# Moving one unit's value products behind other work in TensorE's order, in a two-layer Perceiver-like block

## The chip, the cores and the metric

The kernel runs on 1 core of one Trainium2 chip. The metric is the device time of one execution in microseconds (us). Three executions of the kernel before took 1425.46, 1426.5 and 1429.1 us, a median of 1426.5 us.

## The reference, cut to what matters

The input is 128 batches of 32 tokens of width 256, with a context of 257 keys per batch. Six sub-layers follow each other, each on a layer norm of the running sum and each added to it. Only the names matter below:

```
x = x + cross_attention_0(norm(x), ctx)     # "cross0", one head, 257 keys
x = x + self_attention_0(norm(x))           # "self0", causal, 32 keys
x = x + quantised_feed_forward(norm(x))     # "ffn", 256 -> 1024 -> 256, gelu
x = x + cross_attention_1(norm(x), ctx)     # "query1"/"x1": 16 heads of 16, 257 keys
x = x + local_attention(norm(x))            # "self1": window of 5 among 32 keys
x = x + routed_experts(norm(x))             # "router", then 8 experts, 2 per token
```

The last layer counts tokens per expert in token order and drops those over a capacity. The kernel therefore first writes a table in DRAM that says which token stands where in which expert's queue, and then works off the queues in blocks of 128 rows.

## The kernel before, in words

**Tiles.** Four batches of 32 tokens make a tile of 128 rows, and there are 32 tiles. `stack_phase` takes all tiles through the first five layers and through the router. `expert_phase` then runs the experts and is not touched.

**Units.** The sixteen-head cross-attention of a tile is worked in four units, one for each batch of the tile. For each unit TensorE makes scores (`unit_scores`, L1252, 16 products), VectorE their row maxima (`unit_max`, L1788), ScalarE the exponentials (`unit_probs`, L1426), TensorE the transposes of these (`unit_probs_T`, L1260), ScalarE their copy to SBUF (L1430), and TensorE the value products (`unit_values` and `values_of`, L1263 to L1283: 64 pairs of a weight load and a product on the line L1271, each product only 17 columns wide). Then VectorE adds the last key's part (`unit_own`, L815) and inverts the row sums (`unit_inverse`, L821), GpSimd scales (`unit_scaled`, L933), and VectorE turns the block (`unit_turned`, L825). The units are numbered 0 to 3, so "the fourth unit" is unit 3.

**The order is written out by hand.** Every engine has a function `slot(s)`, which is unrolled for every s in `SLOTS`, and which lists the steps of this engine for several tiles at once: `at(s + 2, step)` does the step for tile s + 2. A round of TensorE holds 505 products in its steady state. Engines meet only at semaphores; `W(engine, signal, tile, step)` waits for one, and each engine works strictly in its own order. The slots are in L1285 (TensorE), L1444 (ScalarE), L1583 (GpSimd) and L1820 (VectorE). `W_bank` waits until the readers of a PSUM bank are done.

**Banks around the change.** Unit 2's values go to bank 6, unit 3's to bank 5. Bank 6 is taken by `c0_norm_T` (L1096, product line L1100) after `unit_own(s, 2)`. Bank 5 is taken by `s0_norm_T` (L1163, product line L1167) after `unit_own(s, 3)`. `s1_v_scores` (L758) makes the second self-attention's value product (line L714, `w_a_Wv`) and its scores (line L765) in bank 7, and needs `ff_gelu1` of tile s + 2 to be done there.

**GpSimd's order.** In its slot stand one after the other `unit_scaled` for units 2 and 3, `scatter_behind` (L1568, L1591; in some of the slots it issues two indirect DMAs from `write_entry`, line L1566, that write a tile's entries of the table), `unit_last(0)` (L1550, `x_lastv`), two bias additions (L913), `ro_rstd` (L923, L1595; `inverse_std`, lines L907 and L909), another bias addition for cross0 (L913).

**Who waits for it.** VectorE's `ro_norm` (L871, line L797, at L1868 in the slot) needs `ro_rstd`. It stands ahead of `s1_x5` and of `s1_x` (L827, line L830, at L1872). `s1_x` frees bank 4 for TensorE's `ro_logits` (L779, at L1288, line L714 with `router`), which stands third in TensorE's next slot, ahead of the next scores:

```
def ro_logits(t):
    W(pe, act_s["router"], t, "normT")
    W_bank(pe, (t + 3, (dve_s["self1_in"], "x")), ...
```

and the quantiser's scale on VectorE, which the change moves too, is

```
def ff_hidden_scale(t):
    W(dve, act_s["ffn"], t, "gelu1")
    row_scale("ffn", t, 1, hid)      # L1740, L1742, L1744, L1745
```

Of the kernel before, what the change touches and what calls it, by code (L numbers as in the profile page):

```python
# [490 lines left out]
def stack_phase(nc, first, t_in, const, logits, ps, constants, consts_loaded, zero, contexts, w2, w2_in, table, table_in, tab_i, places, places_in, rt,  # L491
# [206 lines left out]
    def at(t, step, *unit):  # L698

        name = step.__name__  # L700
        left = CLOSING.get(name, int(name in ("unit_own", "unit_inverse", "unit_scaled", "unit_turned") and unit[0] >= 2))
        if 0 <= t < tiles - left:
            step(t, *unit)
# [256 lines left out]
    with nc.Block() as block:  # L960
# [88 lines left out]
        def _(pe):  # L1049
# [235 lines left out]
            def slot(s):  # L1285
                at(s, unit_probs_T, 1, 1)
                at(s + 1, ff_hidden_T)
                at(s - 4, ro_logits)  # L1288
                at(s + 2, s0_scores)
                at(s, unit_scores, 2)  # L1290
                at(s + 3, c0_scores)
                at(s, unit_values, 0)
                at(s + 1, ff_down)
                at(s, unit_probs_T, 2, 0)
                route_counts(s - 1)
                at(s + 3, c0_probs_T)
                at(s + 2, s0_values)
                at(s, unit_probs_T, 2, 1)
                at(s + 2, s0_out)
                at(s, unit_scores, 3)  # L1300
                at(s + 1, q1_norm_T)
                at(s + 3, c0_values)
                at(s, unit_values, 1)
                at(s + 1, q1_q)
                at(s - 1, s1_norm_T)
                at(s + 3, c0_att_T)
                at(s - 3, ro_norm_T)
                at(s, unit_probs_T, 3, 0)
                at(s, unit_probs_T, 3, 1)
                at(s + 3, c0_out)  # L1310
                at(s + 2, ff_in_T)
                at(s - 1, s1_q)
                at(s + 2, ff_up0)
                at(s + 2, ff_up1)
                at(s + 1, unit_scores, 0)
                at(s, unit_values, 2)
                at(s, unit_values, 3)
                at(s - 1, s1_v_scores)
                at(s + 4, c0_norm_T)
                at(s + 1, unit_probs_T, 0, 0)  # L1320
                at(s + 3, s0_norm_T)
                at(s + 1, unit_probs_T, 0, 1)
                at(s + 4, c0_q)
                at(s + 1, unit_scores, 1)
                at(s + 3, s0_qkv)
                at(s, s1_out)
                at(s - 1, s1_values)
                at(s + 1, unit_probs_T, 1, 0)

            for s in SLOTS:  # L1330
                slot(s)
# [282 lines left out]
        def _(dve):  # L1614
# [180 lines left out]
            def routing(s, j):  # L1795

                first_turn = [rv.best, rv.shifted, rv.first_key, rv.first_top, rv.first_hot, rv.rest, rv.second, rv.second_key]
                second_turn = [rv.second_rank, rv.second_top, rv.second_hot, rv.run_0, rv.run_1, rv.run_2, rv.run_3, None]
                third_turn = [rv.sum, rv.share, rv.where, rv.second_share, rv.held, rv.kept, rv.both, rv.gate]
                fourth_turn = [rv.both_columns, rv.address, rv.address_sum, rv.whole, rv.column, rv.column_f, rv.place, None]  # L1800
                for turn, steps in enumerate((first_turn, second_turn, third_turn, fourth_turn)):
                    g = group_at(s, turn)
                    if g is not None and steps[j]:
                        if steps[j] == rv.where and g == IN_FIRST - 1:
                            next(first_table)
                        steps[j](g, *GROUPS[g])
                        if steps[j] == rv.where:
                            rv.carry(g, *GROUPS[g])
                if (s, j) > (TOTAL_AT, 2) and (s, j) < (TABLE_AT, 2):
                    next(first_table, None)  # L1810
                if (s, j) == (TABLE_AT, 2):
                    rv.rows(0, bank(B["rw"]), tab_i[0])

            def first_from(u):
                if u == 0:
                    dve.wait_ge(places_in[0], 16)
                column = dve.value_load(tab_i[0][0:1, bass.ds(u + P, 1)], min_val=0, max_val=EXP * tiles)
                v_.tensor_copy(first.from_ix[u][:], places[0][:, column, 0:1]).then_inc(first.from_ok.handle, 1)

            def slot(s):  # L1820
                at(s, unit_own, 0)
                at(s + 1, ff_x)
                at(s, unit_inverse, 0)
                at(s + 1, q1_moments)
                routing(s - 1, 2)
                at(s + 3, c0_inv)
                at(s - 1, s1_norm)
                at(s, unit_turned, 0)
                at(s + 1, q1_norm)
                at(s + 2, s0_x)  # L1830
                at(s, unit_max, 3, 0)
                at(s + 2, ff_moments)
                at(s, unit_max, 3, 1)
                at(s + 3, c0_att)
                at(s, unit_own, 1)
                at(s + 2, ff_norm)
                at(s, unit_inverse, 1)
                routing(s - 1, 3)
                at(s + 2, ff_quantise_in)
                at(s + 4, c0_norm)  # L1840
                at(s + 3, c0_x)
                routing(s - 1, 4)
                at(s + 3, s0_moments)
                at(s + 5, c0_moments)
                at(s, unit_turned, 1)
                at(s - 1, s1_qT)
                at(s + 3, s0_norm)
                at(s + 1, unit_max, 0, 0)
                at(s + 1, unit_max, 0, 1)
                at(s, unit_own, 2)  # L1850
                at(s, unit_own, 3)
                at(s, unit_inverse, 2)
                at(s, unit_inverse, 3)
                at(s + 2, ff_hidden_scale)
                at(s, unit_turned, 2)
                at(s - 1, s1_masked)
                if s == tiles - 2:
                    first_from(0)
                    first_from(1)
                at(s + 2, ff_quantise_hidden)  # L1860
                at(s + 1, unit_max, 1, 0)
                at(s, unit_turned, 3)
                at(s - 1, s1_turned)
                routing(s - 1, 5)
                at(s + 1, unit_max, 1, 1)
                at(s - 1, s1_inv)
                routing(s - 1, 6)
                at(s - 2, ro_norm)  # L1868
                at(s - 1, s1_x5)
                routing(s - 1, 7)  # L1870
                routing(s, 0)
                at(s, s1_x)  # L1872
                at(s, s1_moments)
                at(s - 1, ro_moments)
                at(s - 3, ro_logits)
                routing(s, 1)
                at(s + 3, s0_masked)
                at(s + 1, unit_max, 2, 0)
                at(s + 1, unit_max, 2, 1)
                at(s + 4, c0_max)  # L1880
                at(s + 3, s0_scaled)

            for s in SLOTS:
                slot(s)
# [522 lines left out]
```

## Time and profile before

| what | value |
|---|---|
| median of three executions | 1426.5 us |
| the profiled execution | 1423.56 us |
| its span, first to last instruction | 1421.7 us |
| mean granted TensorE clock | 0.985 |
| busy: TensorE / its weight loads | 95% / 80% |
| busy: VectorE, ScalarE, GpSimd | 61%, 55%, 46% |
| TensorE's first and last value product (L1271) | 80.7 us, 882.1 us |

The profile is of one execution. Its own time is 1.9 us over its span, which lies around the span, and 2.9 us under the median of the three. Shares of busy time are means over two phases. From about 60 to 890 us the stack phase runs, in which four engines work side by side; after it the experts' products fill TensorE alone. The change lies in the first.

### The profile page before, as it was taken

Reading aid. Unit: us, or ns where it says so; the run is one execution under the profiler, and the core shown is the slowest. Engines: PE = TensorE matmul, PEld = TensorE weight load, DVE = VectorE, ACT = ScalarE, POOL = GpSimd, SP = SyncE. Lnnn points to the kernel's source line nnn. Section 1 sums busy time; section 2 is a strip of 40 time slices with the busy share of each in tenths; the row PEclk is TensorE's granted clock in tenths of the full one; section 3 lists DMA queues with packets and bytes.
Section 4 is the critical chain, followed back from the end, with each engine's and each line's share of the span. In section 5 each row is a group of like instructions: output and inputs, shape, how many; then the busy total and the mean of one; then the engine's idle time right before and its main releaser. Section 6 shows DMA issues by size and latency. Waiting matters only on the chain. (4 is left out here: it accounts for less than half of the span.)

```text
span 1421.7 us, 51433 instructions
## 1 busy us (share of the span) xinstructions
PE 1344.6 (95%) x19870; PEld 1133.9 (80%) x19903; DVE 863.1 (61%) x3111; ACT 780.4 (55%) x1855; POOL 647.8 (46%) x1195
## 2 busy tenths in 40 slices
PE   8789999999999988999999978999999999999996
PEld 6467777777777767777777756899999999999995
DVE  5679999999988878899999965333111111111110
ACT  1588888888877777888888865321111111111111
POOL 1234444443454545554555543466544434443442
PEclk9899999999999999999999988999999999999999
DMA  9424444343433333343333314666666666666662
GB/s 328 162 75 117 124 114 125 106 125 105 120 117 93 115 111 98 103 134 105 115 108 106 112 69 149 220 182 186 174 178 178 188 182 180 184 184 184 181 181 56
DMA packets 91179, 201.77 MB, mean 142 GB/s; under 512 B 13568, under 2 KB 48128, under 8 KB 79840
## 3 DMA queue, kind: packets, MB, share of 16 engines
q1 hardware_dynamic: 72304, 176.97, 38.4%
q0 software_dynamic: 15680, 18.69, 7.4%
q10 hardware_dynamic: 2992, 3.28, 0.7%
q8 instruction: 142, 2.33, 0.7%
q14 instruction: 61, 0.50, 0.1%
HBM read 180.88 MB, written 18.29 MB: 140 GB/s over the span
## 5 line engine op out<-in xcount | busy, mean ns | idle before, releaser
L2165 ACT ACTIVATE heT<-ps 128x512 f32<-128x512 f32 x142 | 84.7, 597 | 412.0 <-PE ps L2091 383.5
L2091 PEld LDWEIGHTS ps<-xeT,w_block 128*128 128x128 f32 x2272 | 264.6, 192 | 3.7 <-issue 0.2
L2091 PE MATMUL ps<-xeT,w_block 128*128 128x128 f32 x2272 | 266.1, 275 | 0.0
L2078 PE MATMUL ps<-contexts,heT 128*128 x1136 | 257.5, 379 | 1.6 <-DVE ye L1972 1.6
L1426 ACT ACTIVATE x_prob<-ps,x_nmax 128x257 f32<-128x257 f32 x512 | 210.7, 473 | 67.3 <-DVE x_nmax L1788 64.3
L2078 PEld LDWEIGHTS ps<-contexts,heT 128*128 128x128 f32 x1136 | 210.1, 190 | 27.5 <-issue 2.0
L1788 DVE TENSOR_REDUCE x_nmax<-ps 128x2 f32<-128x514 f32 x256 | 169.2, 682 | 15.8 <-PE ps L1252 14.1
L1260 PE MATMUL ps<-constants,x_prob 128*128 128x128 f32 x1024 | 153.1, 281 | 8.4 <-ACT x_prob L1426 7.2
L1430 ACT ACTIVATE x_probT<-ps 128x512 f32<-128x512 f32 x256 | 147.0, 622 | 10.6 <-PE ps L1260 6.3
L1971 DVE COPY to_ix<-places 128x1 uint32 x71 | 10.9, 154 | 231.5 <-PE ps L2078 223.0
L2206 POOL TENSOR_TENSOR rt_hold<-constants 128x1 f32<-128x1 f32 x143 | 34.4, 240 | 225.3 <-DVE ye L1972 124.2
L1260 PEld LDWEIGHTS ps<-constants,x_prob 128*128 128x128 f32 x1024 | 120.1, 144 | 21.0 <-ACT x_prob L1426 14.4
L933 POOL TENSOR_TENSOR x_scaled<-x_own,x_rinv 128x64 f32<-128x64 f32 x128 | 36.3, 294 | 207.4 <-DVE x_rinv L821 207.0
L2212 POOL DMA_INDIRECT out<-ye,to_ix x71 | 113.0, 1591 | 28.5 <-issue 24.0
L1271 PEld LDWEIGHTS ps<-contexts,x_probT 128*32 128x32 f32 x8192 | 90.2, 110 | 39.7 <-ACT ffn_hidden L1396 15.2
L1271 PE MATMUL ps<-contexts,x_probT 128*32 128x17 f32 x8192 | 93.1, 186 | 12.3 <-issue 10.8
L1252 PE MATMUL ps<-contexts,query_blocks 32*64 32x257 f32 x2048 | 89.0, 403 | 11.3 <-ACT x_probT L1430 8.9
L1990 DVE COPY xeT<-ps 128x256 f32<-128x256 f32 x71 | 30.1, 424 | 85.5 <-PE ps L2069 85.4
L2209 POOL DMA_INDIRECT xe<-xnorm,from_ix x69 | 69.0, 1000 | 22.4 <-issue 20.3
L1550 POOL TENSOR_TENSOR x_lastv<-contexts,x_prob 128x68 f32<-128x68 f32 x128 | 44.1, 344 | 60.7 <-ACT x_prob L1426 60.3
L1252 PEld LDWEIGHTS ps<-contexts,query_blocks 32*64 32x64 f32 x2048 | 30.2, 130 | 44.4 <-ACT x_probT L1430 28.1
L907 POOL TENSOR_TENSOR self_var_eps<-self_moments,epsilon 128x1 f32<-128x1 f32 x64 | 12.1, 189 | 88.9 <-DVE self_moments L793 88.9
(280 smaller groups left out, 2714.4 us busy)
## 6 DMA issues: line engine op xcount, KB each, us to landing
w_block<-in_m_w SPq DMA_DIRECT2D x71, 1024.0 KB
contexts<-in_cn SPq DMA_DIRECT2D x112, 272.0 KB
contexts<-in_cT SPq DMA_DIRECT2D x112, 257.0 KB
contexts<-in_m_w SPq DMA_DIRECT2D x8, 1024.0 KB
contexts<-in_cn SPq DMA_DIRECT2D x4, 1088.0 KB
contexts<-in_lastk SPq DMA_DIRECT2D x32, 136.0 KB
contexts<-in_cT SPq DMA_DIRECT2D x4, 1028.0 KB
xin<-in_x SPq DMA_DIRECT2D x32, 128.0 KB, 2.1
```

Of the source, the lines that this page charges most:

```text
L1252: i = mm(ps[h * HS:(h + 1) * HS, r, 0:KEYS], qblk[t % 2][r * GD:(r + 1) * GD, h, u, :, :].rearrange("p e q -> p (e q)"), cT[t % RING][r * ...
L1260: i = tr(ps[:, r, n * P:(n + 1) * P], p1[u % 2][:, r, n * P:(n + 1) * P], ident[:])
L1271: i = mm(b[rows_of, r * DH1:(r + 1) * DH1], p1T[u % 2][:, r, n, rows_of], cn_heads[t % RING][:, u, n, column, :], start=n == 0, stop=n == ...
L1426: A(p1[u % 2][:, r, :], ps[:, r, 0:KEYS], ACT.Exp, bias=nmax1[u % 2][:, r:r + 1]).then_inc(e1_ok.handle, 1)
L1430: A(p1T[u % 2][:, 2 * j:2 * j + 2].rearrange("p r k t -> p r (k t)"), ps[:, 2 * j:2 * j + 2, 0:KT * P], ACT.Copy).then_inc(t1_ok.handle, 1)
L1550: tt(lastv[u % 2][:].rearrange("p (r d) -> p r d", r=RG), lastk[t % RING][:, u, :].rearrange("p (r d) -> p r d", r=RG), p1[u % 2][:, :, KE ...
L1788: v_.tensor_reduce(nmax1[u % 2][:, 2 * j:2 * j + 2], ps[:, 2 * j:2 * j + 2, 0:KEYS], AX, ALU.max, negate=True).then_inc(m1_ok.handle, 1)
L2078: t = mm(ps[:, 3, 0:D], heT[b][:, k, :], w2[:, e, k, :], start=k == 0, stop=k == FK - 1)
L2091: t = mm(ps[:, half, at:at + P], w1[b][:, k, f * P:(f + 1) * P], xeT[b][:, k, :], start=k == 0, stop=k == H - 1)
L2165: A(heT[b][:, half * FK // 2:(half + 1) * FK // 2, :].rearrange("p k t -> p (k t)"), ps[:, half, :], ACT.Gelu).then_inc(heT_ok.handle, 1)
L2209: g.indirect_dma_start(xe[b][:], None, sources[round_of(u, n)], bass.IndirectOffsetOnAxis(ap=from_ix[b][:], axis=0)).then_inc(xe_in[b], 16)
L2212: g.indirect_dma_start(sums[round_of(u, n)], bass.IndirectOffsetOnAxis(ap=to_ix[b][:], axis=0), ye[b][:], None, compute_op=ALU.add).then_i ...
```

## The change

In TensorE's slot unit 3's values stand three steps later, behind `s1_v_scores` and `c0_norm_T`. In VectorE's slot the quantiser's scale of the hidden layer, `ff_hidden_scale`, stands earlier, between `unit_own` of unit 2 and `unit_own` of unit 3, where it stood behind both `unit_own` and both `unit_inverse`. Nothing is added or removed, and GpSimd, ScalarE and the DMA queues keep their order.

```
--- before.py
+++ after.py
@@ -1314,9 +1314,9 @@
                 at(s + 2, ff_up1)
                 at(s + 1, unit_scores, 0)
                 at(s, unit_values, 2)
-                at(s, unit_values, 3)
                 at(s - 1, s1_v_scores)
                 at(s + 4, c0_norm_T)
+                at(s, unit_values, 3)
                 at(s + 1, unit_probs_T, 0, 0)
                 at(s + 3, s0_norm_T)
                 at(s + 1, unit_probs_T, 0, 1)
@@ -1848,10 +1848,10 @@
                 at(s + 1, unit_max, 0, 0)
                 at(s + 1, unit_max, 0, 1)
                 at(s, unit_own, 2)
+                at(s + 2, ff_hidden_scale)
                 at(s, unit_own, 3)
                 at(s, unit_inverse, 2)
                 at(s, unit_inverse, 3)
-                at(s + 2, ff_hidden_scale)
                 at(s, unit_turned, 2)
                 at(s - 1, s1_masked)
                 if s == tiles - 2:
```

## Rows read from the trace of the kernel before

**Rows 1.** DMA queues from 113.95 to 803.72: packets, MB, share of 16 engines.
```profile
q8 instruction: 109, 1.79, 1.0%
```

**Rows 2.** Four stretches: length, busy time (instructions) per engine, granted clock, DMA.
```profile
113.95:286.50 172.55, 169.03 (x3526) 133.12 (x3534) 158.15 (x534) 146.81 (x370) 81.43 (x181) 1.00 0.40 117
286.50:387.27 100.77, 96.98 (x2026) 77.23 (x2029) 91.86 (x336) 85.34 (x214) 45.91 (x105) 1.00 0.39 115
387.27:604.62 217.35, 198.86 (x4050) 157.29 (x4057) 185.87 (x671) 171.55 (x427) 110.19 (x227) 0.98 0.35 108
604.62:803.72 199.10, 195.43 (x4052) 154.23 (x4059) 186.80 (x685) 170.44 (x427) 106.21 (x225) 1.00 0.35 109
```

**Rows 3.** The third of them, L1201 alone (two products per round), PE's first.
```profile
387.27:604.62 217.35, 2.21 (x16) 0.91 (x17) 0.98 0.35 108
```

**Rows 4.** The fourth of them, L1566 alone: GpSimd's scatters, busy (count).
```profile
604.62:803.72 199.10, 16.67 (x16) 1.00 0.35 109
```

**Rows 5.** Waits of PE from 387.27 to 604.62: us in total, times, longest.
```profile
PE ps L1271 <- issue: 9.3, 6, 1.9
```

**Rows 6.** Timeline of PE, 525.4 to 532: start, us, instructions, [idle before <-releaser].
```profile
525.45 0.69 PE L1252 MATMUL ps<-contexts,query_blocks 32*64 32x257 f32 x16
526.18 1.25 PE L1271 MATMUL ps<-contexts,x_probT 128*32 128x17 f32 x116
529.03 0.31 PE L1271 MATMUL ps<-contexts,x_probT 128*32 128x17 f32 x12 [1.61 <-issue]
```

**Rows 7.** DMA from 526.5 to 527.8 in 40 slices, the instruction queue's one packet alone.
```profile
GB/s 0 504 0 0 0 0 0 0 0 0 0 0 0 0 0 0 0 0 0 0 0 0 0 0 0 0 0 0 0 0 0 0 0 0 0 0 0 0 0 0
```

**Rows 8.** Timeline of PE around the last such gap, 580.9 to 583.3.
```profile
583.07 0.38 PE L1271 MATMUL ps<-contexts,x_probT 128*32 128x17 f32 x23 [0.89 <-issue]
```

**Rows 9.** Timeline of PE in an undisturbed round, 187.5 to 194.2.
```profile
190.44 1.33 PE L1271 MATMUL ps<-contexts,x_probT 128*32 128x17 f32 x128
191.70 1.13 PE L714 MATMUL ps<-w_a_Wv,self_normT 128*128 128x256 f32 x4
...
193.30 0.63 PE L1260 MATMUL ps<-constants,x_prob 128*128 128x128 f32 x4
193.77 0.38 PE L1167 MATMUL ps<-constants,self_norm 128*128 128x128 f32 x2
```

**Rows 10.** Timeline of DVE in the round of rows 9.
```profile
191.93 0.35 DVE L815 TENSOR_TENSOR x_own<-ps,x_lastv 128x68 f32<-128x68 f32 x2
...
192.41 1.19 DVE L1740 TENSOR_REDUCE ffn_absmax<-ffn_hidden 128x1 f32<-128x1024 f32 x1
...
194.01 0.23 DVE L825 STREAM_TRANSPOSE x_outT<-x_scaled 128x64 f32<-128x64 f32 x1
```

**Rows 11.** Timeline of POOL, 655 to 667, a round with scatters.
```profile
659.23 0.55 POOL L933 TENSOR_TENSOR x_scaled<-x_own,x_rinv 128x64 f32<-128x64 f32 x2 [1.84 <-DVE x_rinv L821]
...
662.46 0.74 POOL L1550 TENSOR_TENSOR x_lastv<-contexts,x_prob 128x68 f32<-128x68 f32 x1
...
664.85 0.57 POOL L909 TENSOR_TENSOR router_rstd<-router_var_eps,minus_half 128x1 f32<-128x1 f32 x1
...
666.47 0.30 POOL L1550 TENSOR_TENSOR x_lastv<-contexts,x_prob 128x68 f32<-128x68 f32 x1 [0.36 <-ACT x_prob L1426]
```

**Rows 12.** Timeline of all engines, 615 to 618, another such round.
```profile
615.05 0.57 POOL L909 TENSOR_TENSOR router_rstd<-router_var_eps,minus_half 128x1 f32<-128x1 f32 x1
...
615.60 0.71 POOL L913 TENSOR_TENSOR cross_x_bias<-xin,r_x_bv 128x256 f32<-128x256 f32 x1
...
615.72 0.75 DVE L797 TENSOR_SCALAR x_norm<-x,router_moments,router_rstd 128x256 f32<-128x256 f32 x1
...
617.14 0.42 DVE L830 TENSOR_TENSOR x<-ps,x_bias 128x256 f32<-128x256 f32 x1
...
617.71 0.47 PE L714 MATMUL ps<-router,router_normT 128*128 128x8 f32 x3
```

**Rows 13.** Timeline of PE, 764 to 768: a wait that the trace shows.
```profile
767.08 0.58 PE L714 MATMUL ps<-router,router_normT 128*128 128x8 f32 x4 [0.23 <-DVE x L830]
```

More of the change, by code:

```diff
@@ L1316, in slot @@
                 at(s, unit_values, 2)
-                at(s, unit_values, 3)
                 at(s - 1, s1_v_scores)
                 at(s + 4, c0_norm_T)
+                at(s, unit_values, 3)
                 at(s + 1, unit_probs_T, 0, 0)
@@ L1850, in slot @@
                 at(s, unit_own, 2)
+                at(s + 2, ff_hidden_scale)
                 at(s, unit_own, 3)
@@ L1853, in slot @@
                 at(s, unit_inverse, 3)
-                at(s + 2, ff_hidden_scale)
                 at(s, unit_turned, 2)
```

## The prediction
> **What bounds the kernel now.** I read the busy times of stretches first, then TensorE's waits, then the timelines of single rounds. In the stack phase TensorE is busy 98% of 113.95 to 286.50 us and again of 604.62 to 803.72 us [rows 2]. It is TensorE's own order that bounds these rounds. The stretch from 387.27 to 604.62 has 8 rounds (two products of L1201 in each [rows 3]), and the last one, with the same number of products, has 8 too [rows 2]. There a round takes 199.10 / 8 = 24.89 us. The eight rounds before it take 217.35: 18.2 us more for the same work, at a granted clock of 0.98 instead of 1.00, so a little of it at the lower level of 1.2 GHz [rows 2].
>
> That surplus has a place. Six times TensorE stands idle inside the value products of units 2 and 3, 9.3 us in all, and no semaphore ended it [rows 5]. In one such round 116 of the 128 products run, then there is a gap of 1.61 us, then 12 [rows 6]; in the last of the six the gap comes ahead of the last 23 [rows 8]: it creeps through the code from round to round, as a fixed count of instructions would. I read it as a refill of the instruction stream. From 113.95 to 803.72 the instruction queue moves 109 packets of 1.79 MB in all, 16.4 KB each [rows 1], for 13,654 products and 13,679 weight loads [rows 2]: 251 in a packet, and I take 256, since TensorE's waits are not in these rows. One packet starts at 526.53, behind the values' start at 526.18, and TensorE goes on at 529.03 [rows 6, 7]. Counting back 256 instructions from there (232 in the 116 pairs, the rest in the scores ahead) one comes to about 525.5. So a block takes about 3.5 us from the moment its predecessor is entered, and TensorE used up a block in 527.43 - 525.5 = 1.9 us. The two units back to back are 256 instructions in 1.33 us [rows 9]. Nothing else in a round is so dense.
>
> **What the change does to the gaps.** The products between the two units take 193.30 - 191.70 = 1.60 us for 44 instructions [rows 9]. The densest 256 instructions are then unit 2 (0.65), these (1.60) and two thirds of unit 3 (0.43): 2.7 us against 1.3. Where a block begins ahead of unit 2, as in the six rounds of [rows 5], the 0.73 from the scores to the values comes on top in part, 3.3 us against 3.5. (That 0.73 is 526.18 - 525.45 [rows 6].) The gap that is left, 0.2 us, comes ahead of unit 3's end, where VectorE is not ready before 0.3 later (below). The other two rounds keep some 0.6 each. I take 1.2 us as left of 18.2, so **17.0 us go**. Bounds: 9.3 (the visible gaps alone) and 18.2. From 286.50 to 387.27 four rounds have milder gaps, 100.77 against 4 x 24.70, and their blocks begin inside unit 2, where 0.8 us stays; **-0.5**.
>
> The Trainium skill (Runtime: NRT & Kernel Launch, section Instruction fetch mechanics) says that code is refilled in blocks of 16 KiB, two held at a time, and that the fetch is hidden since issue is slower than the fill. The block size agrees with [rows 1]. That it is hidden does not, by the 1.61 us gap. By that sentence the gaps are something else and the 17.0 us stay.
>
> **What it costs at the same place.** VectorE now does the scale of the hidden layer between the two `unit_own`. That is 194.01 - 192.41 = 1.60 us [rows 10]. So `unit_own(3)`, both inverses and what GpSimd waits for come 1.60 later than now. Unit 3's products end 2.9 us after unit 2's start (0.65 + 1.60 + 0.65), that is 193.34 in the round of [rows 9], and `unit_own(3)` starts at 191.93 + 0.14 + 1.60 = 193.67 [rows 10] (0.14 is its distance from the first now), so the scale hides them with 0.3 us to spare. `s0_norm_T` wants bank 5 at 193.77 [rows 9]; `unit_own(3)` ends at 193.88, plus a tenth for the signal: TensorE waits 0.2. Part of that is taken up by ScalarE's chain behind it, but `unit_turned(2)` now waits for GpSimd a little. I take 0.2 per round, between 0 and 0.35, for the 11 rounds from 113.95 to 387.27: **+2.2 us**. `s1_v_scores`, now straight behind unit 2, needs the second gelu, which is done while unit 2 runs: nothing, and if it is late its 0.1 or less shows there.
>
> **What it costs later.** This is the large term. In the 16 rounds with a pair of scatters' issue (16 issues in the last stretch's 8 rounds [rows 4], and as many in the one before) GpSimd is full. It starts scaling at 659.23 and comes to `x_lastv` at 662.46, 3.23 later, and from there to the end of `router_rstd` it takes 2.96, or 2.5 if `x_lastv` takes its 0.30 and not 0.74 [rows 11]. Starting 1.60 later, `router_rstd` ends at 666.6 to 667.0 instead of 665.42. In [rows 12] `ro_norm` begins 0.10 behind that end already now, so there is no slack. It takes 0.75 beside the bias addition that GpSimd starts at 615.60. `s1_x` follows, and TensorE's router product comes 617.71 - 615.62 = 2.09 behind the end of `router_rstd`. For the round of [rows 11] this is 666.6 + 2.0 = 668.6 at the middle of it, against 665.42 + 2.1 = 667.5 now. TensorE already waits for `s1_x` there, 0.23 us [rows 13], and the next scores, maxima and exponentials are behind it, so the delay is paid in full. **1.0 us per round**; from 0.5 (`ro_norm` not held up) to 1.5 (`x_lastv` held up too and 2.09 throughout). With the round after 803.72, 17 rounds: **+17.0 us**. Rounds without scatters have GpSimd free at that point and pay nothing of this.
>
> The rule of the Trainium skill (SBUF — State Buffer, section SBUF: two separate sides) on the port pair that VectorE and GpSimd share, the later one blocking until the first is done, agrees with the 0.75 beside the 0.71 of GpSimd.
>
> **The end of the phase** has one more gap in unit 2 or 3; I take -1.0, from -2 to +1.
>
> **Sum:** -17.0 - 0.5 + 2.2 + 17.0 - 1.0 = +0.7 us. The profiled execution would take 1423.56 + 0.7 = 1424.3, the median 1426.5 + 0.7 = **1427.2 us**. About 0.3%, 4.3 us, is what a measurement of this kernel can tell from no change, so I forecast no difference.
>
> **Rivals.**
> - *The delay on GpSimd costs half.* The gaps go, and `ro_norm` runs unhindered, 0.5 per round: 1427.2 - 8.5 = **1418.7**. For it: the router's product of [rows 11]'s round came 2.1 behind `router_rstd` with the same steps between, so some of them waited for something else. Against: [rows 12, 13]. Chance 0.27.
> - *The router's chain takes the place of the gaps, at 1.5.* VectorE's and GpSimd's operations block each other in the new alignment; from 1.25 us per round this decides, and 17 x 0.5 more gives 1427.2 + 8.5 = **1435.7**, slower. For it: the bias addition is one of several that can collide. Against: `x_lastv` takes 0.30 elsewhere [rows 11]. Chance 0.19.
> - *The change doesn't do what it should: the gaps stay.* If they are no refill, or a refill needs far over 3.5 us, 17.0 stays: 1427.2 + 17.0 = **1444.2**; with half of it, 1435.7. For it: the packet's start [rows 7] explains 1.0 of the 3.5 us, and I don't see the rest. Against: the count of 256. Chance 0.10.
> - *The forecast,* both large terms within 4 us of each other: chance 0.44.
>
> **The numbers.** Faster 0.27, same 0.44, slower 0.19 + 0.10 = 0.29. Both signs hold over half, so the likeliest case's own range is 1423 to 1431. The range of 8 in 10 takes in the first two rivals' values: 1418 to 1435.5, with less than 2 in 10 outside, the third rival most of it.
>
> **What the profile after would show.** Right: rounds from 387 on of one length, about 25.9 us; no idle time of 1.5 us at L1271, `issue` waits of a few tenths at most; a new wait of TensorE for VectorE `x` L830 of about 1 us in every round with scatters, and `router_rstd` ending 1.1 to 1.6 later than now; early rounds of 24.9 us instead of 24.7; `s0_norm_T` (L1167) waiting 0.2 us for `x_own`. Wrong: rounds with scatters near 25.2 (first rival), or over 26.2 (second); gaps of a microsecond moved elsewhere (third); or a wait for ScalarE's exponentials that I costed at nothing, since `s1_masked` comes later on VectorE.

## The result and the profile after

The changed kernel takes 1437.34 us, a median of four executions (1435.88 to 1438.1), beside 1425.98 for the kernel before in the same runs. The ratio is 1.0079, with a 95% interval of 1.0054 to 1.0104. I forecast 1427.2, no difference, and a range up to 1435.5. It became slower, and the range missed it.

The head of the profile page of the changed kernel:

```profile
span 1436.3 us, 51465 instructions
PE 1356.5 (94%) x19902; PEld 1132.2 (79%) x19903; DVE 874.2 (61%) x3111; ACT 780.6 (54%) x1855; POOL 640.7 (45%) x1195
```

The busy times of its four stretches, which answer to [rows 2]: length, busy time and instructions of PE, PEld, DVE, ACT and POOL, granted clock, DMA share, GB/s. A round runs from one first product of L1201 to the next, and I number them, so that these stretches are rounds 2 to 8, 9 to 12, 13 to 20 and 21 to 28:

```profile
116.96:293.24 176.28, 171.94 (x3532) 133.50 (x3533) 161.49 (x534) 147.41 (x371) 81.34 (x181) 1.00 0.41 114
293.24:396.06 102.82, 99.01 (x2031) 77.49 (x2029) 94.49 (x336) 85.45 (x214) 46.65 (x105) 1.00 0.39 113
396.06:607.32 211.26, 199.35 (x4058) 155.31 (x4057) 188.06 (x671) 171.26 (x427) 104.32 (x227) 1.00 0.37 110
607.32:818.16 210.84, 200.81 (x4060) 155.61 (x4059) 187.89 (x685) 170.62 (x427) 103.77 (x225) 0.99 0.34 103
```

Against [rows 2] the stretches are 3.73, 2.05, -6.09 and 11.74 us longer. Another 3.01 us lie ahead of round 2, which begins at 116.96 and not at 113.95. In the thirteen traces of this case beside the changed one it begins anywhere from 112.57 to 118.78, whatever the order of the loop, so I count nothing of these 3 us to the change. After round 28 it is 0.16. That makes the 14.6 us between the two spans. The medians are only 11.4 us apart, since the profiled execution of the kernel before was 2.4 us under the median of its four.

TensorE's waits in the third and in the fourth stretch (us in total, times, longest), to be held against [rows 5]:

```profile
PE ps L714 <- DVE x_outT L825: 4.2, 6, 0.7
PE ps L1271 <- issue: 2.5, 5, 1.1
...
PE ps L714 <- DVE x_outT L825: 4.1, 6, 0.7
PE ps L1260 <- ACT x_prob L1426: 2.2, 4, 1.0
PE ps L714 <- DVE x L830: 2.1, 4, 0.8
```

The gaps at L1271 shrank from 9.3 us to 2.5. In their place TensorE waits for VectorE and ScalarE: 8.4 us in the fourth stretch, where all its waits came to 1.2 before, and 7.4 in the third, where it had waited 3.9 for ScalarE and nothing for VectorE. Before, these rounds were bound by TensorE; now VectorE with GpSimd sets them.

The early rounds show the plainest part of it. These are the groups of three VectorE lines in rounds 4 to 8, before and then after (durations in ns min/median/max, first and last start):

```profile
L1750 DVE TENSOR_SCALAR ffn_hidden<-ffn_hidden,ffn_qscale x5: 771/772/776, 170.2 to 269.0; 128x1024 f32<-128x1024 f32 x5
L1752 DVE TENSOR_SCALAR ffn_hq<-ffn_hidden x5: 1098/1102/1104, 171.0 to 269.8; 128x1024 bf16<-128x1024 f32 x5
L854 DVE TENSOR_TENSOR self_probT<-self_prob_turned,constants x5: 629/633/634, 172.9 to 271.7; 128x128 f32<-128x128 f32 x5
```

```profile
L1750 DVE TENSOR_SCALAR ffn_hidden<-ffn_hidden,ffn_qscale x5: 1253/1254/1261, 174.2 to 275.2; 128x1024 f32<-128x1024 f32 x5
L1752 DVE TENSOR_SCALAR ffn_hq<-ffn_hidden x5: 1096/1100/1103, 175.5 to 276.5; 128x1024 bf16<-128x1024 f32 x5
L854 DVE TENSOR_TENSOR self_probT<-self_prob_turned,constants x5: 634/636/639, 177.5 to 278.5; 128x128 f32<-128x128 f32 x5
```

L1750 went from 0.77 to 1.25. The timelines of GpSimd and then VectorE at that place of the changed kernel (start, us) show why:

```profile
199.46 0.73 POOL L913 TENSOR_TENSOR x_bias<-x,r_x_bo 128x256 f32<-128x256 f32 x1
200.15 1.18 POOL L913 TENSOR_TENSOR self_x_bias<-x,r_a_bv 128x256 f32<-128x256 f32 x1
...
199.49 1.25 DVE L1750 TENSOR_SCALAR ffn_hidden<-ffn_hidden,ffn_qscale 128x1024 f32<-128x1024 f32 x1
200.78 1.10 DVE L1752 TENSOR_SCALAR ffn_hq<-ffn_hidden 128x1024 bf16<-128x1024 f32 x1
```

GpSimd's addition begins 0.03 ahead of L1750, the second addition waits for L1750, and L1752 waits for the second addition. Each holds the other up. In the kernel before the addition began half a microsecond ahead of L1750, and cost it 0.03 at most (0.77, against 0.74 in e4 below):

```profile
194.35 0.73 POOL L913 TENSOR_TENSOR x_bias<-x,r_x_bo 128x256 f32<-128x256 f32 x1
...
194.86 0.77 DVE L1750 TENSOR_SCALAR ffn_hidden<-ffn_hidden,ffn_qscale 128x1024 f32<-128x1024 f32 x1
```

### The profile page after: what moved, and what is told of

The parts are those of the page before. It is cut to its first block and busy times, and to the rows that moved or that the text cites. A ratio compares the mean times of both kernels' runs of the same rounds, so it can differ in the third digit from the quotient of the medians.

```text
span 1436.3 us, 51465 instructions
## 1 busy us (share of the span) xinstructions
PE 1356.5 (94%) x19902; PEld 1132.2 (79%) x19903; DVE 874.2 (61%) x3111; ACT 780.6 (54%) x1855; POOL 640.7 (45%) x1195
## 3 DMA queue, kind: packets, MB, share of 16 engines
q8 instruction: 142, 2.33, 0.7%
## 5 line engine op out<-in xcount | busy, mean ns | idle before, releaser
L1260 PE MATMUL ps<-constants,x_prob 128*128 128x128 f32 x1024 | 153.5, 279 | 12.8 <-ACT x_prob L1426 11.4
L1260 PEld LDWEIGHTS ps<-constants,x_prob 128*128 128x128 f32 x1024 | 118.4, 143 | 25.6 <-ACT x_prob L1426 20.3
L1271 PEld LDWEIGHTS ps<-contexts,x_probT 128*32 128x32 f32 x8192 | 92.0, 110 | 38.7 <-ACT ffn_hidden L1396 15.3
L1271 PE MATMUL ps<-contexts,x_probT 128*32 128x17 f32 x8192 | 98.0, 186 | 6.3 <-issue 4.6
L1252 PE MATMUL ps<-contexts,query_blocks 32*64 32x257 f32 x2048 | 89.6, 405 | 6.7 <-ACT x_probT L1430 4.8
L1252 PEld LDWEIGHTS ps<-contexts,query_blocks 32*64 32x64 f32 x2048 | 30.2, 131 | 38.7 <-ACT x_probT L1430 20.3
L1550 POOL TENSOR_TENSOR x_lastv<-contexts,x_prob 128x68 f32<-128x68 f32 x128 | 40.9, 319 | 35.3 <-ACT x_prob L1426 34.8
```

The costliest lines, as they stand in the source:

```text
L1252: i = mm(ps[h * HS:(h + 1) * HS, r, 0:KEYS], qblk[t % 2][r * GD:(r + 1) * GD, h, u, :, :].rearrange("p e q -> p (e q)"), cT[t % RING][r * ...
L1260: i = tr(ps[:, r, n * P:(n + 1) * P], p1[u % 2][:, r, n * P:(n + 1) * P], ident[:])
L1271: i = mm(b[rows_of, r * DH1:(r + 1) * DH1], p1T[u % 2][:, r, n, rows_of], cn_heads[t % RING][:, u, n, column, :], start=n == 0, stop=n == ...
L1550: tt(lastv[u % 2][:].rearrange("p (r d) -> p r d", r=RG), lastk[t % RING][:, u, :].rearrange("p (r d) -> p r d", r=RG), p1[u % 2][:, :, KE ...
```

## The experiments

Three groups of kernels ran, four in each, and each group beside its own runs of the kernel before: 1420.9 us (19 runs), 1418.93 (16) and 1423.86 (25). So ratios are compared, and stretches of rounds within the profiles.

**One part of the change at a time.**

```
# e1: TensorE's part alone            # e2: VectorE's part alone
 at(s, unit_values, 2)                 at(s, unit_own, 2)
-at(s, unit_values, 3)                +at(s + 2, ff_hidden_scale)
 at(s - 1, s1_v_scores)                at(s, unit_own, 3)
 at(s + 4, c0_norm_T)                  at(s, unit_inverse, 2)
+at(s, unit_values, 3)                 at(s, unit_inverse, 3)
                                      -at(s + 2, ff_hidden_scale)
```

> TensorE's move alone, VectorE's order as before. Theory A (the gaps at L1271 come from the density of instructions, and the cost of the change comes from VectorE's and GpSimd's later start): no idle of 1 us or more at L1271 from 440 to 600 us, since TensorE's order is that of the changed kernel. unit_own(3) waits for unit 3's products (about 1.35 later than before), the scale comes behind it, so everything on VectorE behind it is 1.3 later than before and 0.3 to 0.5 later than in the changed kernel, while GpSimd's scaling starts 0.3 earlier than there. Early rounds 25.4 to 26.0 us (before 24.70, changed 25.24), the whole 1437 to 1450, I take 1443. Rival B (TensorE's move is what costs, VectorE's is harmless): as slow as the changed kernel, 1437, with early rounds of 25.24. Rival C (VectorE's move costs, TensorE's gives the 17 us): 1410.

> VectorE's move alone, TensorE's order as before. Theory A: the gaps at L1271 stay (6 in 387 to 610, 9 us in sum), early rounds 25.2 (unit_own(3) at 5.99 behind the round's first L1201 as in the changed kernel, L1750 beside GpSimd's bias at 1.25 instead of 0.77), rounds with scatters 26.1; the sum of both would be 1437.3 + 17 = 1454, less what of a gap hides beside the scale on VectorE: 1444 to 1454, I take 1449. Rival B (TensorE's move is what costs): about as before, 1426 to 1430.

TensorE's part alone: 1440.7 us, 1.0150 (1.0121 to 1.0179). VectorE's part alone: 1441.95, 1.0162 (1.0133 to 1.0191). The gaps go with TensorE's part (1.6 us in all are left at L1271 from 380 to 610 us) and stay without it (9.6 us, 6 times), as expected. Rivals B and C fall: each part costs about as much alone as both do together. With TensorE's part alone `unit_own(3)` has to wait for the products (VectorE stands idle 1.45 us for L1271 in each early round) and the scale comes behind it, so VectorE is late all the same. The early rounds took 25.2 and not 25.4 to 26.0; L1750 misses the addition there and takes 0.76. So an early round can lose its half microsecond by this wait as well as by the collision. The second kernel came out 7 us under my 1449. Its rounds 13 to 20, with all the gaps, take 214.67 us, only 3.6 more than in the second trace of the changed kernel (211.06, shown with e5):

```profile
396.46:611.13 214.67, 198.59 (x4051) 157.19 (x4058) 190.14 (x671) 170.99 (x427) 107.10 (x227) 0.98 0.36 109
```

While VectorE and GpSimd set the rounds, idle time of TensorE is nearly free. Removing it was worth 3.6 us there, not 17.

**The order on GpSimd, first tries.** I had taken something else for the cause: in the trace of the changed kernel the end of `unit_scores(1)` reaches VectorE 1.27 us late when GpSimd is issuing the second scatter (shown in the last section). Both kernels are the changed one with its GpSimd slot reordered.

```
# e3                                  # e4
-scatter_behind(s, s + 1, 3)           scatter_behind(s, s + 1, 3)
 at(s + 2, unit_last, 0)               at(s + 2, unit_last, 0)
 at(s + 2, q1_bias)                   +at(s - 1, ro_rstd)
 at(s, s1_bias)                        at(s + 2, q1_bias)
 at(s - 1, ro_rstd)                    at(s, s1_bias)
+scatter_behind(s, s + 1, 3)          -at(s - 1, ro_rstd)
```

> The changed kernel with the pair of scatters behind ro_rstd instead of ahead of x_lastv. Theory A (in rounds with scatters the signal of unit_scores(1) reaches VectorE 1.27 late while GpSimd issues the second scatter, and this holds up unit_max(1,0), x_outT and s1_out): VectorE's wait of 1.3 for L1252 ahead of L1788 is gone, unit_max(1,0) starts at 9.5 as in the early rounds instead of 10.03; router_rstd ends at about 10 instead of 12.1; rounds 21 to 28 take 25.2 to 25.6 (now 26.4 on average), unless the scatters now delay another signal of TensorE as much; the whole 1423 to 1431, I take 1427. Rival D (the router's chain alone costs it, the late signal is a bystander): the same fall, since it too is cured here. Rival E (any place costs the same, since the scatters hold up some signal wherever they stand): 1435 to 1439.

> The changed kernel with ro_rstd ahead of the two bias additions on GpSimd; the scatters stay. Theory A: early rounds fall from 25.24 to 24.9, as L1750 takes 0.77 again with no bias addition beside its start; router_rstd ends 1.4 earlier in every round; but the rounds with scatters keep VectorE's wait of 1.3 for L1252 and unit_max(1,0) at 10.03, and fall by 0.2 at most, to 25.9 to 26.2: 11 x 0.34 + 17 x 0.2 = 7 less, 1430. Rival D (the router's chain alone): rounds with scatters fall by about 1.0 to 25.2, the whole to 1437 - 17 - 4 = 1416.

The scatters later: 1425.71, 1.0037 (1.0011 to 1.0063). `ro_rstd` first: 1420.05, 1.0015 (0.9994 to 1.0035), 10 us less than theory A gave and 4 more than theory D. So A was wrong: what the change costs on GpSimd is the order behind the scatters. What I had not expected is the size of the gain in the early rounds. The same three lines in rounds 4 to 8 of e4:

```profile
L1750 DVE TENSOR_SCALAR ffn_hidden<-ffn_hidden,ffn_qscale x5: 743/745/746, 168.8 to 266.2; 128x1024 f32<-128x1024 f32 x5
L1752 DVE TENSOR_SCALAR ffn_hq<-ffn_hidden x5: 694/695/696, 169.6 to 267.0; 128x1024 bf16<-128x1024 f32 x5
L854 DVE TENSOR_TENSOR self_probT<-self_prob_turned,constants x5: 307/308/709, 171.4 to 269.1; 128x128 f32<-128x128 f32 x5
```

All three are shorter, by 0.51, 0.41 and 0.33, and rounds 2 to 8 take 171.33 us instead of 176.28. That is less than in the kernel before (172.55), which paid for the second and the third of them all along. In the rounds with scatters of e4 the chain had a new end, the bias for `s1_x5` (VectorE's timeline, idle time and its releaser in brackets):

```profile
632.61 0.48 DVE L865 SCALAR_TENSOR_TENSOR x<-ps,self_rinv,self_x_bias 128x256 f32<-128x256 f32 x1 [0.79 <-POOL self_x_bias L913]
```

**Both kernels again, and the order that this asks for.** No trace of e1 to e4 had the late signals. So I traced both kernels once more, and gave both the same new order on GpSimd:

```
# e5: the changed kernel, e6: the kernel before, neither edited
# e7: the changed kernel, e8: the kernel before, both with
-scatter_behind(s, s + 1, 3)
 at(s + 2, unit_last, 0)
-at(s + 2, q1_bias)
+at(s - 1, ro_rstd)
 at(s, s1_bias)
-at(s - 1, ro_rstd)
+scatter_behind(s, s + 1, 3)
+at(s + 2, q1_bias)
```

> The changed kernel itself, once more, beside the kernel before in the same runs. In the traces of the first four experiments no signal of TensorE is late (none over 0.3 us), while the traces of the kernel before and of the changed kernel have 41 to 72 such signals. Theory F (the late signals belong to the occasion on which these two were traced, and not to the change): none here, the wait of 1.3 for L1252 ahead of L1788 is gone, unit_max(1,0) at 9.5 or earlier in rounds with scatters; their rounds take 25.7 to 26.2 (they were 26.4 on average), and the ratio to before is 1.003 to 1.010, I take 1.006. Theory A (the late signal is the change's own, from the scatter under unit_scores(1)): it is there again and the ratio is 1.008 or more.

> The kernel before itself, once more. Theory F: no late signals of TensorE, while the gaps at L1271 from 440 to 610 us are there as before (6, 9 us in sum), since they come from the order of instructions; early rounds 24.70, rounds 21 to 28 24.9. Theory A: late signals as in the first trace.

> The changed kernel with GpSimd's slot reordered: x_lastv, ro_rstd, s1_bias, then the pair of scatters, then q1_bias. Theory G (what the change costs is wholly GpSimd's chain, first ro_rstd, then the bias that s1_x5 needs, and L1750 beside a bias addition): early rounds 24.35 as in the run with ro_rstd first; router_rstd ends at 8.7 and s1_bias at 9.5 in every round; rounds with scatters 24.4 to 24.9; rounds 13 to 20 without idle of 1 us at L1271; the whole 1403 to 1412, I take 1407. Rival H (VectorE's later order itself costs, whatever GpSimd does): rounds with scatters stay at 25.3 or more, the whole 1416 to 1422.

> The kernel before with the same reordering of GpSimd's slot. Theory G: the gaps at L1271 stay, 6 of them, about 9 us, so the run is 8 to 15 us above the one with the change and this order; GpSimd's chain was not the bound before, so little falls: early rounds 24.3 to 24.7, the whole 1414 to 1421, I take 1418. Rival I (the order on GpSimd is worth as much without the change, and TensorE's move brings nothing): as fast as the changed kernel with this order.

e5 took 1438.09 us, 1.0132 (1.0091 to 1.0172); e6 took 1415.33 in its one execution. Neither has late signals, so theory F was right on that, but my ratio of 1.003 to 1.010 was not: without them it is the kernel before that becomes faster. Rounds 13 to 20 and 21 to 28 of e6, then the same of e5:

```profile
387.43:598.93 211.50, 196.88 (x4050) 156.16 (x4057) 187.98 (x671) 171.10 (x427) 107.85 (x227) 0.99 0.36 110
598.93:798.64 199.71, 195.84 (x4052) 154.30 (x4059) 187.96 (x685) 170.29 (x427) 106.52 (x225) 1.00 0.36 109
```

```profile
394.74:605.80 211.06, 198.84 (x4050) 156.00 (x4057) 188.67 (x671) 171.09 (x427) 104.42 (x227) 0.99 0.37 111
605.80:817.60 211.80, 200.33 (x4052) 156.31 (x4059) 190.56 (x685) 170.66 (x427) 103.82 (x225) 0.98 0.33 103
```

The kernel before loses 211.50 - 199.71 = 11.8 us in rounds 13 to 20, and not the 18.2 of [rows 2]. The changed kernel takes the same in both traces. And here stands the chain that I had forecast, in a round with scatters of e5 (GpSimd, then VectorE, then TensorE; idle time and its releaser in brackets):

```profile
646.95 0.57 POOL L909 TENSOR_TENSOR router_rstd<-router_var_eps,minus_half 128x1 f32<-128x1 f32 x1
...
647.63 0.75 DVE L797 TENSOR_SCALAR x_norm<-x,router_moments,router_rstd 128x256 f32<-128x256 f32 x1 [0.80 <-POOL router_rstd L909]
...
648.76 0.41 DVE L830 TENSOR_TENSOR x<-ps,x_bias 128x256 f32<-128x256 f32 x1
...
649.32 0.58 PE L714 MATMUL ps<-router,router_normT 128*128 128x8 f32 x4 [0.61 <-DVE x L830]
```

`router_rstd` ends 12.14 behind the round's beginning (635.38), against 11.01 in e6. VectorE stands idle for it, the addition of `cross_x_bias` holds up L797 (0.75), and TensorE waits at the router's product as in [rows 13], but for 0.61, and 15 times in the phase (12.7 us in all, 1.5 at most).

e7 took 1409.34, 0.9930 (0.9902 to 0.9958); e8 took 1424.42, 1.0034 (1.0010 to 1.0057). So with this order on GpSimd the change is worth 15.1 us, where with the old order it costs 19.2. The stretches of rounds 2 to 8, 13 to 20 and 21 to 28 of e7 and then of e8:

```profile
117.96:289.29 171.33, 168.78 (x3525) 133.12 (x3533) 154.21 (x534) 147.26 (x371) 79.45 (x181) 1.00 0.41 118
...
391.68:593.92 202.24, 195.62 (x4051) 155.05 (x4058) 184.98 (x671) 171.04 (x427) 106.92 (x227) 1.00 0.38 116
593.92:795.51 201.59, 195.64 (x4052) 154.62 (x4059) 186.31 (x685) 170.37 (x427) 106.36 (x225) 1.00 0.36 108
```

```profile
118.78:290.70 171.92, 168.91 (x3526) 133.16 (x3533) 157.63 (x534) 147.09 (x371) 80.89 (x181) 1.00 0.40 117
...
392.19:606.42 214.23, 198.67 (x4050) 158.40 (x4057) 185.28 (x671) 171.17 (x427) 106.11 (x227) 0.98 0.36 109
606.42:809.19 202.77, 196.23 (x4052) 154.80 (x4059) 191.29 (x685) 170.16 (x427) 107.74 (x225) 1.00 0.35 107
```

The difference of 12.0 us in rounds 13 to 20 is the gaps and what follows on them, and this is the pair that shows their worth: the other two stretches differ by 0.6 and 1.2, and rounds 9 to 12 by 0.9 the other way. The gaps that show at L1271 from 380 to 610 us are 10.4 us in e8 and 1.5 in e7. In three of these rounds of e8, 18 to 20, the mean granted clock is 0.94, and in none of e7. I put the rest down to that; no run separates the two. Theory G held for the sum, and H and I fall. But rounds with scatters take 25.2 and not 24.4 to 24.9, which is near the 25.3 of H. Its reason is not VectorE's later order, since rounds 21 to 28 of e8, with the old one, take 25.3 too. One reason, in three of the sixteen rounds (15, 19 and 23), is in VectorE's timeline, a tiny operation between two additions of GpSimd that takes 0.15 in the same rounds of e5:

```profile
656.23 1.22 DVE L350 TENSOR_TENSOR rt_entries<-rt_gate,rt_kept 128x8 f32<-128x8 f32 x1
```

For the kernel before this order is no gain (I expected 1418): the additions meet other operations of VectorE. In rounds 21 to 28 its L797 takes 0.86 to 0.98, against 0.40 to 0.76 in e6.

**Which collision, another place for the additions, and another cure for the gaps.**

```
# e9: the changed kernel               # e10: the changed kernel
 scatter_behind(s, s + 1, 3)          +at(s + 2, q1_bias)
 at(s + 2, unit_last, 0)              +at(s, s1_bias)
 at(s + 2, q1_bias)                    at(s + 1, unit_scaled, 2)
+at(s - 1, ro_rstd)                    at(s + 1, unit_scaled, 3)
 at(s, s1_bias)                       -scatter_behind(s, s + 1, 3)
-at(s - 1, ro_rstd)                    at(s + 2, unit_last, 0)
                                      -at(s + 2, q1_bias)
                                      -at(s, s1_bias)
                                       at(s - 1, ro_rstd)
                                      +scatter_behind(s, s + 1, 3)

# e11: the kernel before, unit 2 in bank 5 and unit 3 in bank 6
 at(s - 1, s1_q)
+at(s, unit_values, 2)
 at(s + 2, ff_up0)
 at(s + 2, ff_up1)
 at(s + 1, unit_scores, 0)
-at(s, unit_values, 2)
# e12: e11 with the GpSimd slot of e10
```

> The changed kernel with ro_rstd between the two bias additions: scatters, x_lastv, q1_bias, ro_rstd, s1_bias. So q1_bias still starts beside L1750, while router_rstd ends 0.7 earlier than in the changed kernel. Theory J (the early rounds' 0.5 comes from L1750 held up by the bias addition beside it): L1750 keeps 1.25, unit_max(1,0) at 9.52 and early rounds of 25.0 to 25.2. Theory K (it comes from router_rstd being late): early rounds of 24.5 to 24.7, halfway or more to the 24.35 of the run with ro_rstd first. Rounds with scatters in both: router_rstd at 11.4, s1_x 0.5 to 0.7 earlier, 25.3 to 25.7; the whole 1425 to 1432 by J, 1419 to 1426 by K.

> The changed kernel with both bias additions ahead of unit_scaled(2) on GpSimd, then x_lastv, ro_rstd and only then the scatters. GpSimd is idle for 3.4 us at that place. The theory (the change costs only through GpSimd's chain and through additions that hold up VectorE): early rounds 24.3 to 24.4; in rounds with scatters L350 (1.22 beside two bias additions in the last run of the changed kernel) takes its own time, so s1_x ends near 12.7 and these rounds take 24.4 to 25.0 (25.2 in that run); the whole 1402 to 1410, I take 1406. Rival (s1_x waits for TensorE and VectorE themselves): as the run before it, 1409.

> The kernel before with unit 2's products moved forward, behind s1_q and ahead of ff_up0 (units 2 and 3 exchange their banks for it), VectorE and GpSimd as before. The densest 256 instructions now take about 0.65 + 0.8 + 0.7 + 0.45 = 2.6 us instead of 1.3. Theory (the gaps are refills that take about 3.5 us a block): of the gaps of 1.6 to 1.9 us at L1271 half stays, 0.9 at most each and 5 us at most in sum (10.2 before), now in unit 3 alone; rounds 13 to 20 fall from 211.5 to 202 to 207; other rounds within 0.3 of before, as unit_scores(1,0) comes 0.65 later but nothing waits for it at once; the whole 1410 to 1416, I take 1413 (before 1419). Rival L (the gaps are not from density, but from the place of unit 3 behind s1's steps or from something else in the round): gaps and rounds 13 to 20 as before, 1419 or more.

> The same with both bias additions ahead of unit_scaled(2), then x_lastv, ro_rstd and the scatters on GpSimd. If both theories hold: early rounds 24.3 to 24.7, rounds 13 to 20 200 to 205, rounds 21 to 28 24.5 to 25.0, the whole 1403 to 1412, near the best run. If the order on GpSimd brings nothing to an order with VectorE unchanged, as in the run of the kernel before with the reordered slot (1.0034): 1413 to 1420.

e9: 1428.59, 1.0030 (1.0004 to 1.0057). The whole lies in the range of theory J. Its rounds 2 to 8 take 172.15 us, 24.6 each, which is what theory K gave, and yet K's reason is not it. The three lines again:

```profile
L1750 DVE TENSOR_SCALAR ffn_hidden<-ffn_hidden,ffn_qscale x5: 1251/1256/1261, 172.7 to 270.9; 128x1024 f32<-128x1024 f32 x5
L1752 DVE TENSOR_SCALAR ffn_hq<-ffn_hidden x5: 693/694/694, 174.0 to 272.2; 128x1024 bf16<-128x1024 f32 x5
L854 DVE TENSOR_TENSOR self_probT<-self_prob_turned,constants x5: 366/368/370, 175.5 to 273.8; 128x128 f32<-128x128 f32 x5
```

L1750 kept its 1.25, and the other two gave back 0.41 + 0.27 = 0.68 per round, where rounds 4 to 8 gave 0.69 each (25.24 to 24.55). Nor did VectorE wait for `router_rstd` in the early rounds, in either kernel. So it is neither J nor K as I had put them. As long as VectorE sets such a round, its cost is the sum of all collisions on VectorE, and L1750 was only the newest. It ends where TensorE is the bound again: in e4 the three lines gave back 1.25 together and the round 0.89. The rounds with scatters took 26.2, over the 25.3 to 25.7 of both theories; in twelve of the sixteen VectorE waits 1.3 us for a late signal of L1252 (last section).

e10: 1406.82, 0.9884 (0.9854 to 0.9913), the fastest of all, 1.2% under the kernel before and 0.8 us over my 1406. Early rounds came to 24.4 as expected. Rounds with scatters did not fall below those of e7 on average:

```profile
112.66:283.27 170.61, 168.29 (x3525) 133.06 (x3533) 153.37 (x534) 147.68 (x371) 78.77 (x181) 1.00 0.41 118
...
383.52:585.70 202.18, 196.88 (x4051) 155.15 (x4057) 185.04 (x671) 170.94 (x427) 107.81 (x227) 1.00 0.39 116
585.70:789.15 203.45, 196.73 (x4052) 154.87 (x4059) 185.56 (x685) 170.52 (x427) 107.09 (x225) 1.00 0.35 107
```

The theory was right on its own point: L350 takes 0.17 at most, and rounds 15, 19 and 23 fell from 25.6 to 25.8 us in e7 to 24.9 to 25.1. Others rose. In e10 VectorE waits 0.44 to 0.48 us for L1252 in twelve of the sixteen rounds, where it waits 0.14 at most in e7, since signals were late again in this run (last section). Round 24 is one of them, and takes 25.13 us against 24.36 in e7; there L385 takes 0.70 instead of 0.16 as well. What e10 would take without the late signals no run shows.

e11: 1421.17, 0.9974 (0.9955 to 0.9992), over my 1410 to 1416. Its gaps from 380 to 610 us (TensorE's waits), and its rounds 2 to 8 and 13 to 20 (the stretches):

```profile
PE ps L1271 <- issue: 3.0, 4, 1.0
```

```profile
114.20:290.07 175.87, 170.46 (x3525) 133.43 (x3533) 158.81 (x534) 147.12 (x371) 81.64 (x181) 1.00 0.39 115
...
391.53:599.31 207.78, 196.74 (x4051) 155.20 (x4057) 189.43 (x671) 171.08 (x427) 107.93 (x227) 1.00 0.37 112
```

This thins the same stretch of code in another way, with the order on VectorE and GpSimd as before, and the gaps fall from 10.2 us to 3.0, the longest from 1.9 to 1.0: what a fixed refill time of about 3.5 us gives for 256 instructions in 2.6. Rival L falls. Rounds 13 to 20 came to 207.78, a little over my 202 to 207, and keep 4.5 us over rounds 21 to 28 (203.27). I had costed the later `unit_scores(1, 0)` at nothing. VectorE takes its maxima ahead of both `unit_own`, these start 0.57 later, and every early round pays nearly 0.5. e12: 1416.88, 0.9947 (0.9924 to 0.9969). That is not near e10, and inside the range for an order on GpSimd that brings nothing (1413 to 1420), though it is 4.3 us under e11. Rounds 13 to 20 took 207.68 and not 200 to 205, and the early rounds 24.8. This run had late signals too, so the two cures aren't compared on an equal footing.

## Why the prediction was wrong

**The bound.** Right. Rounds 13 to 20 lost their time in the gaps at L1271, and thinning the code in two different ways shrank them about as the count of 256 instructions from [rows 1, 6, 7] gave: to 2.5 us and 0.9 in the two traces of the changed kernel, and to 3.0 in e11. The longest that were left are 1.1, 0.9 and 1.0, where I had forecast a few tenths. The rival that the gaps stay is excluded. That a gap is a refill stays an inference from the count and the packet of [rows 7]; what the runs show is that the gaps go with the density of the code. On the Trainium skill's sentence that the fetch is hidden (Runtime: NRT & Kernel Launch, section Instruction fetch mechanics), e7, e8 and e11 go the way of the rows. The two blocks that the prediction took from that section are its general figure; for TensorE it gives room for 2048 instructions, which no run here tests.

**The gaps, -17.0.** Mis-sized. It measured 12.0 us (e7 against e8), and even that has three rounds at a lower clock in it. Of the 18.2 of [rows 2] the second trace of the same kernel has 11.8; the rest belonged to the occasion of the first one, which had two rounds with a lower clock (15 and 17, one in e6) and late signals. And the term took for granted that TensorE stays the bound. With VectorE late, the same gaps were worth 3.6 us (e2 against e5).

**The cost at the same place, 0.2 per round: this is the step that failed.** It measured 3.73 us over seven rounds, 0.53 each, and 4.1 us over the term of +1.7 for rounds 2 to 12. The step looked for waits of TensorE only, and found one, for bank 5 at L1167, which is real (L1167 starts 6.35 behind the round's beginning instead of 6.07) and is mostly taken up by what follows. It never asked which operations of GpSimd now lie beside which of VectorE. The runs showed in its place L1750 at 1.25 us instead of 0.77 beside GpSimd's addition, 0.48 of the 0.53. I had weighed such a collision at one place, L797, and drawn on the Trainium skill for it (SBUF — State Buffer, section SBUF: two separate sides), by which the later of the two blocks fully. The rows of L1750 agree with it, and so do L1752 and L854 in e4 and e9.

**The cost later, 1.0 per round with scatters.** The mechanism was right, and nearly the size. In e5, whose trace has no late signals, seven of the eight rounds from 605.80 on take 25.6 to 26.5 us, (211.80 - 29.58) / 7 = 26.03 on average, against 199.71 / 8 = 24.96 in e6: 1.07. What I left out is the round of 29.58, and another of 28.95 among rounds 13 to 20. Both fall to the lower clock for a while (last section), which makes the mean 1.5. In the first trace of the changed kernel the surplus is 11.74 / 8 = 1.47, one round of 27.85 among them.

**The end, -1.0.** 0.16 behind round 28, in which round 29 is 2.2 us longer, so the rest gained 2.0. I did not follow it.

**The sum.** By the first pair of traces, forecast against measured: rounds 2 to 12 +1.7 and +5.8; rounds 13 to 20 -9.0 and -6.1; rounds 21 to 28 +8.0 and +11.7; afterwards 0 and +0.2; ahead of round 2 nothing and +3.0. All errors have one sign. The range was said to take in the first two rivals, but its top, 1435.5, lies under the 1435.7 of the second. This rival, the router's chain at 1.5 per round, was nearest in its time, and its condition, operations that block each other in the new alignment, was the true one, in the early rounds more than at its own place.

Open is why the fall to the lower clock comes in some rounds and not in others, and how much of the 25.3 to 25.4 us of e10's rounds with scatters is due to its late signals.

## What to carry to other kernels

When a step moves by a microsecond or two on one engine, list what will then lie beside it on the engine with which it shares a port, for the whole round and not for the one chain under study; here a collision showed as a longer duration (0.77 to 1.25) and not as a wait. A gain on the engine that is the bound is worth its full price only while it stays the bound: here the same edit cost 19 us or brought 15, by the order of five lines on another engine. And a surplus read from one execution should be read from a second one before it carries the sum.

## What the hardware showed that I had not expected

**Late signals.** A signal is what an engine sends at the end of a step to those that wait for it. In the first trace of the changed kernel `unit_scores(1)` (TensorE) ends at 668.84, and VectorE's maximum waits 1.27 us longer. In e5 the same step of another such round goes on at once, 0.11 behind the end of `unit_scores(1)` at 644.09 (TensorE, VectorE, then VectorE of e5):

```profile
668.15 0.69 PE L1252 MATMUL ps<-contexts,query_blocks 32*64 32x257 f32 x16
...
670.15 0.69 DVE L1788 TENSOR_REDUCE x_nmax<-ps 128x2 f32<-128x514 f32 x1 [1.27 <-PE ps L1252]
```

```profile
644.20 0.69 DVE L1788 TENSOR_REDUCE x_nmax<-ps 128x2 f32<-128x514 f32 x1
```

In the two first traces and in e9 to e12, 16 to 51 signals of TensorE per trace come 0.3 to 1.8 us behind the end of their step, and 178 of these 186 while GpSimd was issuing an indirect DMA. In e1 to e8 there are 0 to 5. (The 41 to 72 of an expectation count in steps for which the trace has no signal at all within 3 us.) ScalarE and VectorE have them as well, 17 to 69 each in the same six traces, and 2 at most in the others. So they belong to the occasion and not to the program. The kernel before took 1425.98 and 1423.86 us on occasions with them, and 1420.9 and 1418.93 without. The changed kernel took 1437.34 with them and 1438.09 without: from round 13 to 28 VectorE waits 17.5 us for L1252 in the first trace, and 12.6 us for `router_rstd` in e5. In e9 and e10, where GpSimd's order takes that other wait away, the waits for L1252 are VectorE's largest in these rounds (18.1 and 9.1 us). No run tells what sets the occasion. It is not the chip alone, since e1 to e4 and e9 to e12 are recorded with the same chip number.

**The clock.** Slices of 4 us from e5, in the round of 29.58 us:

```profile
618.00:622.00 4.00, 2.33 (x32) 2.08 (x40) 3.12 (x16) 3.39 (x8) 2.19 (x6) 0.87 0.21 70
622.00:626.00 4.00, 4.00 (x98) 2.18 (x99) 2.64 (x8) 2.22 (x8) 0.21 (x1) 0.50 0.00 0
626.00:630.00 4.00, 3.87 (x30) 2.88 (x35) 2.36 (x13) 1.95 (x5) 1.33 (x5) 0.78 0.47 135
```

TensorE was busy for 2.33 of 4 us, held up by ScalarE's exponentials (1.07) and by `s1_x` (0.80). Towards the end of this slice the granted clock fell to 0.50 of full speed, 1.2 GHz, and stayed there for about 6.8 us (an estimate from the three slices: 1.04 + 4 + 1.76). The round took 29.58 against 26.03 for its neighbours, 3.6 us more, which is about what half speed for 6.8 us costs. In e5 this happened in two of sixteen rounds with scatters. The kernels with the old order of TensorE have it too, in rounds with a gap at L1271: rounds 18 to 20 of e8, with gaps of 1.7 to 1.9 us, each have a mean granted clock of 0.94.
